# Four gather partitions moved from GpSimd to SyncE and ScalarE in three graph convolutions

## Chip, cores and metric

The program runs on one core of a Trainium2 chip. The metric is the device time of one execution in microseconds. The time before is 11902.84 us, the median of two runs (11900.63 and 11905.05).

## What is computed

The program is a chain of four graph layers on 12,500 nodes with 64 features and 200,000 edges, sorted by destination. The change lies in the last layer, three edge convolutions in a row:

```python
def conv(h, W, b):
    m = jnp.concatenate([h[dst], h[src], edge_attr], axis=1) @ W + b
    return jax.ops.segment_sum(m, dst, num_segments=n_nodes)
h = jax.nn.relu(conv(x, W1, b1))
h = jax.nn.relu(conv(h, W2, b2))
return conv(h, W3, b3)
```

What costs is `h[src]`: for each of the 200,000 edges a row of 64 floats (256 bytes) is read from a table in memory at an index that the data give, and the rows are summed by destination.

## The kernel before

**Tiling.** The edges are laid out as 128 partitions of 1,564 columns each (`P` = 128, `J` = 1564). The columns are worked off in 68 chunks (`NC`) of 23 (`C`). For one column GpSimd issues one indirect DMA: 128 indices, one per partition, are read from `g.src`, and 128 rows of the table `tab3` land in the chunk's buffer `rin`. There are two such buffers, used in turn. In these three convolutions that makes 3 x 1,564 gathers; the same helper `gather_columns` (its issue is L864) also serves the two attention layers ahead of them, from other tables.

**The chunk pipeline of `conv_layer`** (k = 0, 1, 2 is the convolution):

- GpSimd gathers chunk after chunk. Before chunk c it waits until chunk c-2 has been taken out of the buffer (`s_rows` in the helper, `s_in` in `conv_layer`), so it may run a chunk ahead of ScalarE.
- ScalarE's `take(c)` prepares the mask `keeps` (L2098), copies the carry column (L2100), waits for the 23 gathers of the chunk, and copies the rows into `chain` with features outermost (L2106; L2105 copies the edge attributes, in the first convolution alone).
- VectorE runs a scan along the columns (L2244), which sums the rows of one destination.
- ScalarE's `give(c)` waits for the scan and copies the sums out (L2111).
- SyncE waits for that copy (the helper at L90) and stores the chunk (L2068). In the first convolution it also loads edge attributes two chunks ahead (L2049, L2050, L2053).
- In the first 33 chunks ScalarE also does small copies for three node tiles per chunk (L2116 to L2130), between `take` and `give`, for a product on TensorE.

**The order of the work.** Each engine's instructions stand in the order of the code and run in that order; between engines semaphores alone order them. At the start of the program SyncE (L384) and ScalarE (L487) load the weights. Among SyncE's are, for each convolution, parts of 64x64, one of 16x64 and the bias of 1x64, from memory into one partition; among ScalarE's are parts of 16x8x16 and 16x8 (`rel_msg`, `rel_pri`). Up to that point SyncE also stores tables in a loop (L414, L422), where a register operation computes the address ahead of each DMA.

Of the kernel before, what the change touches and what calls it, by code (L numbers as in the profile page):

```python
# [25 lines left out]
U32 = mybir.dt.uint32  # L26

P = 128
# [9 lines left out]
NP = T * P  # L38
# [37 lines left out]
BATCH = 3  # L76
UNIT = 8
ARENA = 25600
SEG = 32
SEGS = -(-J // SEG)  # L80
JP = SEGS * SEG
# [108 lines left out]
def pool_sem(g, name):  # L190


    return g.new_pool_sem(name)
# [660 lines left out]
            v.tensor_copy(g.a2row[:, :], ps_w[:, 260:260 + D])  # L854


def gather_columns(pool, table, idx, rows, s_gath, s_rows):

    for c in range(NC):
        b = c % 2  # L860
        wait(pool, s_rows, c - 1)
        for j in range(C):
            at = c * C + j
            pool.indirect_dma_start(out=rows[b][:, j, :], out_offset=None, in_=table,  # L864
                                    in_offset=bass.IndirectOffsetOnAxis(ap=idx[:, at:at + 1].bitcast(U32), axis=0))\
                .then_inc(s_gath[b], 16)

def store_rows(eng, i, b, rows, width, out, s_rows, s_stored):
# [1104 lines left out]
def conv_layer(nc, ctx, g, a, k, out_rows):  # L1973
# [7 lines left out]
        "rows_turned", "rows_copied", "rows_multiplied", "summed", "relu", "out"))  # L1981
    s_ea = [sem(f"attrs{b}") for b in range(2)]
    s_gath = [pool_sem(g, f"gathered{b}") for b in range(2)]
    s_row = pool_sem(g, "fixed_rows")
    s_blank, s_pair = sem("pair_blank"), sem("pair_in")
    paired = k > 0
# [31 lines left out]
    with ExitStack() as inner:  # L2018
# [4 lines left out]
        ps_o = [bank(f"o{b}") for b in range(ring)]  # L2023
        block = inner.enter_context(nc.Block())

        @block.gpsimd
        def _(pool):
            gather_columns(pool, g.tab3, g.src, rin, s_gath, s_in)

            fix = bass.IndirectOffsetOnAxis(ap=g.fix[:, 0:1].bitcast(U32), axis=0)  # L2030
            pool.wait_ge(s_st, 16 * NC)
            pool.indirect_dma_start(out=row, out_offset=None, in_=table_rows, in_offset=fix).then_inc(s_row, 16)
            pool.wait_ge(s_put, 1)
            pool.indirect_dma_start(out=table_rows, out_offset=fix, in_=row, in_offset=None).then_inc(s_row, 16)
            pool.wait_ge(s_row, 32)
            pool.wait_ge(s_last, 1)

            for n, tiles in enumerate(units):
                for t in tiles:
                    ends = bass.IndirectOffsetOnAxis(ap=g.end_i[:, t:t + 1].bitcast(U32), axis=0)  # L2040
                    pool.indirect_dma_start(out=cat[:, t, 0:width], out_offset=None, in_=table_rows, in_offset=ends)\
                        .then_inc(s_end[n], 16)

        @block.sync
        def _(sp):
            def load_attrs(c):
                b = c % 2
                cols = slice(c * C, c * C + C)
                sp.dma_start(ea[b][0:EVEN, :, :], attrs[0:EVEN, cols, :]).then_inc(s_ea[b], 16)  # L2049
                sp.dma_start(ea[b][EVEN:P - 1, :, :], attrs[EVEN:P - 1, cols, :]).then_inc(s_ea[b], 16)  # L2050
                n = min(LAST - c * C, C)
                if n > 0:
                    sp.dma_start(ea[b][P - 1:P, 0:n, :], last_attrs[:, c * C:c * C + n, :]).then_inc(s_ea[b], 16)  # L2053

            if paired:
                wait(sp, s_blank, 1)
                for half in (slice(0, D), slice(D, P)):
                    sp.dma_start(g.Wkv[half, k - 1, half], a[f"L3_gnn_W{k + 1}"][D:2 * D, :]).then_inc(s_pair, 16)
            wait(sp, s_init, 1)
            if k == 0:  # L2060
                for c in range(2):
                    load_attrs(c)
            for c in range(NC):
                wait(sp, s_in, c + 1)
                if k == 0 and c + 2 < NC:
                    load_attrs(c + 2)
                wait(sp, s_copied, c + 1)
                sp.dma_start(dest[:, c * C:c * C + C, :], rows).then_inc(s_st, 16)  # L2068

            n_out = 0  # L2070
            for n, tiles in enumerate(units):
                t0, t1 = tiles.start, tiles.stop
                done = n + 1
                if k < 2:
                    wait(sp, s_relu, done)
                    sp.dma_start(g.tab3.rearrange("(p t) f -> p t f", t=T)[:, t0:t1, :], g.H[:, t0:t1, :])\
                      .then_inc(s_out, 16)
                    n_out += 1
                else:
                    wait(sp, s_sum, done)  # L2080
                    for p0, p1 in ((0, EVEN), (EVEN, P - 1)):
                        sp.dma_start(out_rows[p0 * T:p1 * T, :].rearrange("(p t) f -> p t f", t=T)[:, t0:t1, :],
                                     g.X[p0:p1, t0:t1, :]).then_inc(s_out, 16)
                        n_out += 1
                    if t0 < REST:
                        whole = min(t1, REST)
                        sp.dma_start(out_rows[(P - 1) * T + t0:(P - 1) * T + whole, :].rearrange("(a t) f -> a t f", a=1),
                                     g.X[P - 1:P, t0:whole, :]).then_inc(s_out, 16)
                        n_out += 1
            wait(sp, s_out, 16 * n_out)  # L2090

        @block.scalar
        def _(act):
            def take(c):
                b, cols = c % 2, slice(c * C, c * C + C)
                act.wait_ge(s_init, 2)
                wait(act, s_rows, c)
                nc.scalar.copy(keeps[:, :, 1:C1], g.keep[:, cols].unsqueeze(1).to_broadcast([P, HF, C])).then_inc(s_flags, 1)  # L2098
                if c:
                    nc.scalar.copy(chain[:, :, 0], chain[:, :, C]).then_inc(s_chained, 1)  # L2100
                    act.wait_ge(s_chained, c)
                act.wait_ge(s_gath[b], (c // 2 + 1) * 16 * C)
                if k == 0:
                    act.wait_ge(s_ea[b], 16 * sum(2 + (LAST > x * C) for x in range(b, c + 1, 2)))
                    nc.scalar.copy(chain[:, D:R3, 1:C1], ea[b].rearrange("p j f -> p f j"))  # L2105
                nc.scalar.copy(chain[:, 0:D, 1:C1], rin[b].rearrange("p j f -> p f j")).then_inc(s_in, 1)  # L2106

            def give(c):
                act.wait_ge(s_rows, c + 1)
                wait(act, s_st, 16 * c)  # L2110
                nc.scalar.copy(rows.rearrange("p j f -> p f j"), chain[:, :, 1:C1]).then_inc(s_copied, 1)  # L2111

            def scale(t):
                b = t % 2
                wait(act, s_tr, t - 1)
                ins = nc.scalar.activation(hd[b][:, 0:D], g.H[:, t, :], ACT.Copy, scale=g.deg[:, t:t + 1])  # L2116
                if k:
                    ins = nc.scalar.copy(hd[b][:, D:K17], g.E17[:, t, :])  # L2118
                ins.then_inc(s_scaled, 1)

            def copy_turned(t):
                b = t % 2
                act.wait_ge(s_tr, t + 1)
                wait(act, s_mm, t - 1)
                nc.scalar.copy(ht[b][0:K_Z, 0:P], ps_t[b][0:K_Z, 0:P]).then_inc(s_ht, 1)  # L2125

            def copy_z(t):
                b = t % 2
                act.wait_ge(s_mm, t + 1)
                nc.scalar.copy(z[:, t, :], ps_o[b][:, 0:D]).then_inc(s_z, 1)  # L2130

            scale(0)
            for c in range(NC):
                take(c)
                for t in range(c * BATCH, min(c * BATCH + BATCH, T)):
                    if t + 1 < T:
                        scale(t + 1)
                    copy_turned(t)
                    if t:
                        copy_z(t - 1)  # L2140
                if c * BATCH < T <= c * BATCH + BATCH:
                    copy_z(T - 1)
                give(c)

            def relu(q):
                tiles = units[q]
                act.wait_ge(s_sum, q + 1)
                h = g.H[:, tiles[0]:tiles[-1] + 1, :].rearrange("p t f -> p (t f)")
                nc.scalar.activation(h, h, ACT.Relu).then_inc(s_relu, 1)

            depth = P if paired else K_T
            for q, tiles in enumerate(units):
                n = len(tiles) * P // (2 if paired else 1)
                act.wait_ge(s_ctr, q + 1)
                wait(act, s_cmm, q - ring + 1)
                nc.scalar.copy(ht[q % ring][0:depth, 0:n], ps_t[q % ring][0:depth, 0:n]).then_inc(s_cht, 1)  # L2156
                if q and k < 2:
                    relu(q - 1)
            if k < 2:
                relu(len(units) - 1)  # L2160
# [161 lines left out]
```

## Time and profile before

| | |
|---|---|
| runs, median | 11902.84 us |
| profiled execution, span | 13242.4 us (the program's rows fill it; no time around it is listed) |
| GpSimd busy | 9106.3 us, 69% |
| VectorE busy | 4015.6 us, 30% |
| ScalarE busy | 3476.7 us, 26% |
| TensorE busy | 1352.0 us, 10% |
| gathers at L864 | 7,820, of which 4,692 in the three convolutions |
| one gather in the convolutions | 0.95 us, and 0.30 us to the next |

The profiled execution is longer than the runs: with the recorder on, the program takes 13242.4 us. Rows are compared with rows, and the sum is carried over to the runs by the ratio of the two. A span's share of busy time is a mean over stages. In the three convolutions, from about 6,100 us to the end, one engine is nearly always issuing and the others wait for it most of the time; the rows further down show it.

### The profile page before, as it was taken

Reading aid. Unit: us, or ns where it says so; the run is one execution under the profiler, and the core shown is the slowest. Engines: PE = TensorE matmul, PEld = TensorE weight load, DVE = VectorE, ACT = ScalarE, POOL = GpSimd, SP = SyncE. Lnnn points to the kernel's source line nnn. Section 1 sums busy time; section 2 is a strip of 40 time slices with the busy share of each in tenths; the row PEclk is TensorE's granted clock in tenths of the full one; section 3 lists DMA queues with packets and bytes.
Section 4 is the critical chain, followed back from the end, with each engine's and each line's share of the span. In section 5 each row is a group of like instructions: output and inputs, shape, how many; then the busy total and the mean of one; then the engine's idle time right before and its main releaser. Section 6 shows DMA issues by size and latency. Waiting matters only on the chain. (4 is left out here: it accounts for less than half of the span.)

```text
span 13242.4 us, 37433 instructions
## 1 busy us (share of the span) xinstructions
PE 1352.0 (10%) x6735; PEld 1005.3 (8%) x6735; DVE 4015.6 (30%) x5472; ACT 3476.7 (26%) x4561; POOL 9106.3 (69%) x8728
## 2 busy tenths in 40 slices
PE   5200000020000000395000000200000000000000
PEld 3100000010000000273000000200000000000000
DVE  2255555544445544695111111011111101111110
ACT  2333223312222222375232222122211212221121
POOL 3677777767777776402777777577777767777776
PEclk7655555555555555697555555555555555555555
DMA  7333333313333333001222222111111111111111
GB/s 277 133 97 97 98 95 95 100 34 90 98 95 94 94 99 81 14 1 32 61 58 61 58 58 60 40 50 46 49 46 46 49 39 50 46 49 46 46 49 42
DMA packets 404823, 919.05 MB, mean 69 GB/s; under 512 B 171046, under 2 KB 195277, under 8 KB 389496
## 3 DMA queue, kind: packets, MB, share of 16 engines
q0 software_dynamic: 278944, 386.91, 13.3%
q1 hardware_dynamic: 121832, 529.42, 10.9%
q14 instruction: 175, 1.43, 0.0%
q10 hardware_dynamic: 3824, 0.50, 0.0%
q8 instruction: 48, 0.79, 0.0%
HBM read 456.45 MB, written 459.77 MB: 69 GB/s over the span
## 5 line engine op out<-in xcount | busy, mean ns | idle before, releaser
L864 POOL DMA_INDIRECT arena<-tab,src x6256 | 6549.8, 1047 | 2894.4 <-issue 2101.0
L2244 DVE TENSOR_TENSOR_SCAN arena<-cv_keep,arena 128x768 f32<-128x768 f32 (+1 forms) x476 | 752.0, 1627 | 5757.2 <-issue 4526.3
L864 POOL DMA_INDIRECT arena<-tab,spread x1564 | 1644.1, 1051 | 518.5 <-issue 518.5
L2106 ACT COPY arena<-arena 128x1472 f32<-128x1472 f32 x204 | 545.3, 2673 | 3003.9 <-DMA arena<-tab,src 3003.9
L2111 ACT COPY arena<-arena 128x1472 f32<-128x1472 f32 (+1 forms) x204 | 588.3, 2884 | 551.8 <-DVE arena L2244 431.2
L1089 PE MATMUL e_t<-ident,arena 128*68 128x128 f32 (+1 forms) x2 | 0.8, 397 | 4433.5 <-PEq L1433 2223.3
L2168 PE MATMUL cv_t<-ident,arena 128*81 128x128 f32 (+1 forms) x294 | 137.9, 469 | 2917.7 <-ACT arena L2118 1528.3
L2105 ACT COPY arena<-arena 128x368 f32<-128x368 f32 x68 | 55.3, 813 | 1353.7 <-issue 1325.1
L2182 PE MATMUL cv_t<-ident,arena 128*64 128x128 f32 (+1 forms) x3 | 1.3, 425 | 3391.1 <-ACT arena L2111 3391.1
L951 ACT ACTIVATE ae_prob<-arena 128x92 f32<-128x92 f32 x68 | 17.1, 251 | 1228.8 <-remote 1152.7
L1089 PEld LDWEIGHTS e_t<-ident,arena 128*68 128x68 f32 (+1 forms) x2 | 0.3, 134 | 4433.9 <-issue 4433.9
L1502 DVE TENSOR_TENSOR arena<-arena,ge_small 128x23 f32<-128x23 f32 x68 | 13.3, 195 | 1064.8 <-DMA arena<-tab,src 1064.8
L1883 DVE TENSOR_SCALAR arena<-arena 128x448 bf16<-128x448 f16 x1252 | 324.8, 330 | 37.4 <-PE po_u L1766 20.4
L1766 PE MATMUL po_u<-arena,Hn 128*128 128x448 bf16 x1564 | 300.6, 354 | 291.4 <-DVE Hn L1873 291.4
L1025 DVE TENSOR_TENSOR arena<-arena,ae_prob 128x1472 f32<-128x1472 f32 x68 | 260.1, 3824 | 220.3 <-issue 217.2
L1465 ACT ACTIVATE ge_decay<-arena 128x768 f32<-128x768 f32 x68 | 56.4, 830 | 1015.4 <-issue 944.1
L992 DVE TENSOR_TENSOR_SCAN ae_work<-ae_keep,arena 128x768 f32<-128x768 f32 x136 | 240.1, 1765 | 224.2 <-remote 146.5
L1766 PE MATMUL po_u<-arena 128*128 128x448 bf16 x1564 | 298.9, 352 | 1.0 <-DVE arena L1883 1.0
L943 ACT ACTIVATE ae_work<-arena 128x768 f32<-128x768 f32 x136 | 208.5, 1533 | 300.7 <-DVE arena L1037 287.5
L2168 PEld LDWEIGHTS cv_t<-ident,arena 128*81 128x81 f32 (+1 forms) x294 | 53.9, 184 | 2953.8 <-ACT arena L2118 1538.3
L1034 DVE TENSOR_TENSOR_SCAN arena<-ae_work,arena 128x768 f32<-128x768 f32 x136 | 238.9, 1757 | 115.3 <-ACT ae_work L943 103.4
L1506 DVE TENSOR_TENSOR arena<-arena,ge_small 128x1472 f32<-128x1472 f32 x68 | 258.7, 3805 | 0.2 <-issue 0.2
(370 smaller groups left out, 6943.0 us busy)
## 6 DMA issues: line engine op xcount, KB each, us to landing
rows<-arena SPq DMA_DIRECT2D x68, 1506.5 KB
arena<-tab,src POOLq DMA_INDIRECT x6256
rows3b<-arena SPq DMA_DIRECT2D x136, 736.0 KB
rows<-arena SPq DMA_DIRECT2D x68, 920.0 KB
rows<-arena SPq DMA_DIRECT2D x68, 828.0 KB
tab<-arena SPq DMA_DIRECT2D x49, 1024.0 KB
q_start<-arena SPq DMA_DIRECT2D x32, 1564.0 KB
arena<-q_start SPq DMA_DIRECT2D x68, 736.0 KB
```

The source lines that it names most:

```text
L864: pool.indirect_dma_start(out=rows[b][:, j, :], out_offset=None, in_=table, in_offset=bass.IndirectOffsetOnAxis(ap=idx[:, at:at + 1].bitca ...
L943: return nc.scalar.activation(works.rearrange("p (h d) j -> p h d j", h=HH), args[:, 0, :, h0:h0 + HH].rearrange("p j h -> p h j").unsquee ...
L992: v.tensor_tensor_scan(out=work[:, :], data0=keep[:, :], data1=qts[:, x * HF * C1:(x + 1) * HF * C1], initial=0.0, op0=ALU.mult, op1=ALU.a ...
L1025: v.tensor_tensor(mix[:, :, 1:C1].rearrange("p (h d) j -> p j h d", h=H), kv[:, :, D:2 * D].rearrange("p j (h d) -> p j h d", h=H), prob.u ...
L1034: ins = v.tensor_tensor_scan(out=part, data0=work[:, :], data1=part, initial=0.0, op0=ALU.mult, op1=ALU.add)
L1506: v.tensor_tensor(peak[:, :, 1:C1].rearrange("p f j -> p j f"), r[:, :, D:2 * D], pre.unsqueeze(2).to_broadcast([P, C, D]), ALU.mult).then ...
L1766: ins = nc.tensor.matmul(ps_u[:, x, 0:half], wide[c % 2][:, x * P:x * P + P, j], ring[:, n % RING, :], start=(n == 0), stop=(n == J - 1))
L1883: v.tensor_scalar(ring[:, n % RING, :], iota_hi, hi[:, n:n + 1], None, ALU.is_equal).then_inc(s_hot, 1)
L2106: nc.scalar.copy(chain[:, 0:D, 1:C1], rin[b].rearrange("p j f -> p f j")).then_inc(s_in, 1)
L2111: nc.scalar.copy(rows.rearrange("p j f -> p f j"), chain[:, :, 1:C1]).then_inc(s_copied, 1)
L2168: nc.tensor.transpose(ps_t[b][0:K_Z, 0:P], hd[b][:, 0:K_Z], g.ident[:, :]).then_inc(s_tr, 1)
L2244: ins = v.tensor_tensor_scan(out=part, data0=keep[:, 0:(f1 - f0) * C1], data1=part, initial=0.0, op0=ALU.mult, op1=ALU.add)
```

## The change

A constant gives the number of partitions that GpSimd gathers in each convolution: 127, 124 and 126. The rest are fetched row by row. SyncE takes the first one or two of them, ScalarE what is left: partition 127 by SyncE in the first convolution; 124 and 125 by SyncE, 126 and 127 by ScalarE in the second; 126 and 127 by SyncE in the third. For each partition and chunk, 23 indices are read from `g.src` into registers of the issuing engine, in two instructions (12 and 11), and for each index a DMA brings one row of 64 floats from `tab3` to its place in `rin`. These DMAs signal four semaphores `s_side` in turn, and `take` waits for them too. Chunks 0 and 1 are fetched ahead of the chunk loop, chunk c+2 at the end of chunk c: on SyncE behind the store, on ScalarE behind `give`, after a wait for its own `take`.

```diff
+GATHERED = (127,124,126)
...
+def fetch_rows(nc, eng, engine, table, idx, c, partitions, dest, signal):
+
+    for p in partitions:
+        for j in range(0, C, 12):
+            n = min(12, C - j)
+            _, values = nc.values_load_multi_w_load_instructions(
+                idx[p:p + 1, c * C + j:c * C + j + n], engines=[engine], min_val=0, max_val=NP - 1,
+                skip_runtime_bounds_check_because="row numbers of the edge list, as the indirect gathers use them")
+            for x, value in enumerate(values):
+                eng.dma_start(dest[p:p + 1, j + x, :], table[bass.ds(value, 1), :]).then_inc(signal, 16)
+
-def gather_columns(pool, table, idx, rows, s_gath, s_rows):
+def gather_columns(pool, table, idx, rows, s_gath, s_rows, n=P):
...
-            pool.indirect_dma_start(out=rows[b][:, j, :], out_offset=None, in_=table,
-                                    in_offset=bass.IndirectOffsetOnAxis(ap=idx[:, at:at + 1].bitcast(U32), axis=0))\
+            pool.indirect_dma_start(out=rows[b][0:n, j, :], out_offset=None, in_=table,
+                                    in_offset=bass.IndirectOffsetOnAxis(ap=idx[0:n, at:at + 1].bitcast(U32), axis=0))\
...
+    n_gathered = GATHERED[k]
+    s_side = [sem(f"side{n}") for n in range(4)]
...
+        of_sp = range(n_gathered, min(n_gathered + 2, P))
+        of_act = range(n_gathered + 2, P)
...
-            gather_columns(pool, g.tab3, g.src, rin, s_gath, s_in)
+            gather_columns(pool, g.tab3, g.src, rin, s_gath, s_in, n_gathered)
...
+            for c in range(2):
+                fetch_rows(nc, sp, mybir.EngineType.SP, g.tab3, g.src, c, of_sp, rin[c % 2], s_side[c % 4])
             for c in range(NC):
                 wait(sp, s_in, c + 1)
                 if k == 0 and c + 2 < NC:
                     load_attrs(c + 2)
                 wait(sp, s_copied, c + 1)
                 sp.dma_start(dest[:, c * C:c * C + C, :], rows).then_inc(s_st, 16)
+                if c + 2 < NC:
+                    fetch_rows(nc, sp, mybir.EngineType.SP, g.tab3, g.src, c + 2, of_sp, rin[c % 2], s_side[(c + 2) % 4])
...
                 act.wait_ge(s_gath[b], (c // 2 + 1) * 16 * C)
+                act.wait_ge(s_side[c % 4], (c // 4 + 1) * 16 * C * (P - n_gathered))
...
             scale(0)
+            for c in range(2):
+                fetch_rows(nc, act, mybir.EngineType.Activation, g.tab3, g.src, c, of_act, rin[c % 2], s_side[c % 4])
             for c in range(NC):
                 take(c)
...
                 give(c)
+                if c + 2 < NC:
+                    act.wait_ge(s_in, c + 1)
+                    fetch_rows(nc, act, mybir.EngineType.Activation, g.tab3, g.src, c + 2, of_act, rin[c % 2],
+                               s_side[(c + 2) % 4])
```

ScalarE's rows in the second convolution, late in the chunk loop, before: `give` of a chunk (L2111), then `take` of the next (L2098, L2100, L2106).

```order
L2106 COPY arena<-arena 128x64x23
L2111 COPY arena<-arena 128x64x23
L2098 COPY cv1_keep<-keep 128x32x23
L2100 COPY arena<-arena 128x64
L2106 COPY arena<-arena 128x64x23
L2111 COPY arena<-arena 128x64x23
```

At the same place in the changed program the lines are numbered 22 higher (L2133 is `give`, L2128 the copy of gathered rows); ISA is a register operation, here the one that turns an index into an address.

```order
L2119 COPY cv1_keep<-keep 128x32x23
L2121 COPY arena<-arena 128x64
L2128 COPY arena<-arena 128x64x23
L2133 COPY arena<-arena 128x64x23
L863 TENSOR_LOAD src
L867 ISA
L867 DMA arena<-tab3 1x64
```

After these come the other 45 pairs of ISA and DMA with three more TENSOR_LOADs among them, 96 instructions in all, and then again L2119, L2121 and L2128: they stand between `give` of one chunk and `take` of the next, where nothing stood before.

SyncE's rows in the second and third convolution before were stores alone (L2068, `rows3b<-arena`, 68 in a row). In the changed program the same 96 instructions stand between two stores; this is the place of one store (now L2087) in the second convolution.

```order
L867 ISA
L867 DMA arena<-tab3 1x64
L2087 DMA rows3b<-arena 128x1472
L863 TENSOR_LOAD src
L867 ISA
L867 DMA arena<-tab3 1x64
```

In the first convolution SyncE has half of that, 48 instructions for one partition. GpSimd's order is unchanged; its gathers read and write fewer partitions. SyncE's program grows from 605 listed rows to 17,058 and ScalarE's from 4,260 to 10,788.

## Rows read from the trace of the kernel before

**Rows 1.** Page: span, then busy us (share) and instructions per engine

```profile
span 13242.4 us, 37433 instructions
PE 1352.0 (10%) x6735; PEld 1005.3 (8%) x6735; DVE 4015.6 (30%) x5472; ACT 3476.7 (26%) x4561; POOL 9106.3 (69%) x8728
```

**Rows 2.** Page, costliest groups: count, busy us, mean ns, idle before, releaser

```profile
L864 POOL DMA_INDIRECT arena<-tab,src x6256 | 6549.8, 1047 | 2894.4 <-issue 2101.0
...
L864 POOL DMA_INDIRECT arena<-tab,spread x1564 | 1644.1, 1051 | 518.5 <-issue 518.5
```

**Rows 3.** Timeline of GpSimd, second convolution: start us, us, [idle before <-releaser]

```profile
8999.32 0.95 POOL L864 DMA_INDIRECT arena<-tab,src  x1 [0.30 <-issue]
9000.58 0.95 POOL L864 DMA_INDIRECT arena<-tab,src  x1 [0.30 <-issue]
9001.83 0.95 POOL L864 DMA_INDIRECT arena<-tab,src  x1 [0.30 <-issue]
```

**Rows 4.** Timeline of ScalarE, second convolution, one late chunk

```profile
9710.17 2.67 ACT L2106 COPY arena<-arena 128x1472 f32<-128x1472 f32 x1 [22.60 <-DMA arena<-tab,src]
9716.38 2.67 ACT L2111 COPY arena<-arena 128x1472 f32<-128x1472 f32 x1 [3.54 <-DVE arena L2244]
9718.86 0.87 ACT L2098 COPY cv_keep<-keep 128x736 f32<-128x736 f32 x1
9719.67 0.35 ACT L2100 COPY arena<-arena 128x64 f32<-128x64 f32 x1
9742.38 2.68 ACT L2106 COPY arena<-arena 128x1472 f32<-128x1472 f32 x1 [22.36 <-DMA arena<-tab,src]
```

**Rows 5.** Groups of ScalarE, second convolution (8500 to 10725 us)

```profile
L2111 ACT COPY arena<-arena 128x1472 f32<-128x1472 f32 x68 | 181.9, 2675 | 168.7 <-DVE arena L2244 129.3 <-issue 39.4
L2106 ACT COPY arena<-arena 128x1472 f32<-128x1472 f32 x68 | 181.9, 2674 | 1502.1 <-DMA arena<-tab,src 1502.1
```

**Rows 6.** Timeline of SyncE's queue, one chunk of the first convolution

```profile
7043.69 0.33 SPq L2049 DMA_DIRECT2D arena<-in_edge_attr_dram  x1
7044.06 0.43 SPq L2050 DMA_DIRECT2D arena<-in_edge_attr_dram  x1
7044.54 0.25 SPq L2053 DMA_DIRECT2D arena<-in_edge_attr_dram  x1
7051.39 0.36 SPq L2068 DMA_DIRECT2D rows<-arena  x1
```

**Rows 7.** Waits of SyncE's queue, second convolution: us in total, times, longest

```profile
SPq L90 <- ACT arena L2111: 1016.0, 32, 38.1
```

**Rows 8.** Groups of GpSimd: scatter of 4-byte rows

```profile
L1638 POOL DMA_INDIRECT s_start<-small,start_i x98 | 101.1, 1032 | 29.9 <-issue 29.9
```

**Rows 9.** Timeline of SyncE's queue: bias of 1x64, then 64x64, 64x64, 16x64

```profile
421.95 0.28 SPq L384 DMA_DIRECT2D Wt<-in_L_gnn_b_dram  x1
422.27 0.47 SPq L384 DMA_DIRECT2D Wz<-in_L_gnn_W_dram  x1
422.78 0.60 SPq L384 DMA_DIRECT2D Wt<-in_L_gnn_W_dram  x1
423.42 0.58 SPq L384 DMA_DIRECT2D Wz<-in_L_gnn_W_dram  x1
```

**Rows 10.** The same, in the loop with register operations between DMAs

```profile
197.34 0.34 SPq L422 DMA_DIRECT2D tab<-arena  x1
197.88 0.39 SPq L414 DMA_DIRECT2D q_start<-arena  x1
202.39 0.35 SPq L422 DMA_DIRECT2D tab<-arena  x1
202.96 1.00 SPq L414 DMA_DIRECT2D q_start<-arena  x1
```

**Rows 11.** Timeline of ScalarE's queue: DMAs of 16 partitions

```profile
9.90 0.45 ACTq L487 DMA_DIRECT2D arena<-in_L_gnn_rel_pri_dram  x1
10.38 0.44 ACTq L487 DMA_DIRECT2D arena<-in_L_gnn_rel_att_dram  x1
```

**Rows 12.** A lone gather, and DMA busy tenths in 40 slices of 8342.4:8345.4

```profile
8342.40 0.95 POOL L2032 DMA_INDIRECT arena<-rows,fix  x1 [16.46 <-DMA rows<-arena]
DMA  0000000000000000000006942300000000000000
```

**Rows 13.** DMA of 9048.2:9049.45, one gather: packets; share of 16 engines

```profile
DMA packets 32, 0.03 MB, mean 26 GB/s; under 512 B 16, under 2 KB 16, under 8 KB 32
q0 software_dynamic: 32, 0.03, 13.9%
```

## Prediction

> **What bounds the kernel now.** I read the page first: GpSimd is busy 69% of the span, no other engine over 30% [rows 1]. A GpSimd row of about 1.05 us stands 7,820 times at L864, one per gathered column, and nothing released most of its idle time but its own issue [rows 2]. So the part to look at is `gather_columns`, and there the three `conv_layer` calls, 1,564 gathers each. The timeline of GpSimd shows the beat: a row of 0.95 us, 0.30 us of issue, 1.25 us from one to the next [rows 3]. A chunk of 23 gathers lasts 32.2 us: in the timeline of ScalarE the copy L2106, which waits for a chunk's rows, starts at 9710.17 and at 9742.38 [rows 4]. Between two such copies ScalarE sits idle: 1502.1 us over the 68 chunks of the second convolution, 22.1 us each, all until the gather's DMA lands [rows 5]. SyncE too has nearly the whole chunk free: one store of 0.36 us, in the first convolution three loads of about 1 us together [rows 6], and waits of 1016.0 us at 32 stops, 31.7 us each [rows 7]. So GpSimd sets the time, ScalarE has 22 us a chunk to give and SyncE 31.
>
> **The change, part by part.** All of this is in the profiled execution's time, 13242.4 us; the runs' median is 11902.84, 0.899 of it, and I carry the sum over by that ratio.
>
> *Fewer partitions per gather.* No row of before gathers other than 128 rows. What rows do show is that bytes don't matter: gathers of 512-byte rows take 1051 ns, scatters of 4-byte rows 1032 ns [rows 2, 8]. So the 0.95 us is either fixed for the instruction (gain 0, and I see no reason for a loss but the one under the rivals), or goes by rows: 0.95/128 = 7.4 ns a row, 11.6 us per row over 1,564 gathers. One, four and two rows are taken off: 81 us at the most. With nothing to tell the two apart I take the middle, 3.7 ns a row: 6 us in the first convolution, 12 us in the third; in the second it shortens a chunk by 4 x 23 x 3.7 ns = 0.3 us.
>
> *What a row costs SyncE or ScalarE.* Each is a register operation (ISA) and a DMA of 1x64. SyncE has issued just such a DMA: 0.28 us, the next one 0.32 us after its start [rows 9]. With a register operation before the next DMA the gap behind a DMA grows from 0.04 to 0.20 us: 0.34 us at 197.34, the next at 197.88 [rows 10]. So 0.28 + 0.20 = 0.48 us. ScalarE's shortest DMAs of before are of 16 partitions, 0.44 to 0.45 us each and 0.48 us apart [rows 11], so its row lies between 0.32 us (SyncE's bare spacing) and 0.48 + 0.16 = 0.64; SyncE took 0.58 us for 16x64 [rows 9], so ScalarE isn't the slower issuer, and I take 0.48 for it too.
>
> *Reading the indices.* Two TENSOR_LOADs per row and chunk (12 and 11 numbers). None stands in before. Bounds: 0.16 us, a register operation's gap, and 1.6 us, what a lone gather needs from its start at 8342.40 to its first packet, in slice 22 of the 40 of 75 ns [rows 12]. I take 0.8. The Trainium skill ("DMA: Bandwidth & Descriptors", Latency and other measured facts) gives a floor of about 600 ns for such a load; by it, an estimate, ScalarE's fetch below would be 24.5 us and the forecast 11,900; no run here shows it yet.
>
> *SyncE.* First convolution: 23 x 0.48 + 2 x 0.8 = 12.6 us a chunk beside 1.4 us of its own: hidden in 31.7. Second and third: 46 x 0.48 + 4 x 0.8 = 25.3 us, hidden too, with 6 us left. Its fetch for chunk c+2 stands behind the store of chunk c, a whole chunk ahead of its use.
>
> *ScalarE, second convolution.* The same 25.3 us now stand between `give(c)` and `take(c+1)`. Ahead of `take` nothing else may run, so the keep copy (0.87 us), the carry copy (0.35), the wait for the gather and L2106 all queue behind the fetch; behind L2106 wait DVE's scans, the store, and GpSimd, which may run one chunk ahead. The fetch can start when the copy L2111 is handed over, not when it ends: L2098 starts at 9718.86, before L2111 ends at 9719.05, so the queue runs ahead of the engine [rows 4]. From 9716.38 to 9742.38 are 26.0 us, less 1.2 for the two copies: a window of 24.8 (the same as 22.1 idle + 2.67), and 24.5 with the shorter gathers. The fetch overruns it by 0.8 us. From then on ScalarE sets the beat: 66 chunks x 0.8 = 53 us. The first two fetches, 50.6 us, run before the first `take`, which before came after 32.2: another 18 us that a bound engine does not make up. In the other convolutions ScalarE only gains a wait on a semaphore long passed.
>
> Sum: 13242.4 - 6 - 12 + 53 + 18 = 13295; times 0.899, **11,950 us**, 0.4% more than now.
>
> **The rivals.**
>
> *All of it is hidden.* If a row on ScalarE costs 0.46 us or less, or a load 0.6, the fetch fits and the gathers' gain is left: 0 to 81 us, so 11,830 to 11,903. For it: SyncE's bare spacing of 0.32 [rows 9]. Against: the margin is under 1 us.
>
> *Issue is dearer, and it gets slower.* At 0.64 us a row and 1.6 us a load the fetch is 35.8 us: ScalarE overruns by 11.3 x 66 = 746 us, its start by 40, and SyncE overruns the third convolution's chunk (36.2 against 32) by 4.2 x 66 = 277: 14,299, or 12,850. It is over 2% (265 us) once the fetch takes 28.4 us, at 0.55 us a row. There is another way past 2%: if the recorder slows GpSimd's rows alone and not ScalarE's, the true chunk is 28.9 us, the window 21.2 and the overrun 4.1 x 66 = 271. For it: SyncE's DMAs behind a large one take 1.00 us where they took 0.39 [rows 10], and the fetches stand behind a 736 KB store.
>
> *The gather itself gets slower.* Now a gather is 16 data packets, 32 with the semaphore writes, and 13.9% of 16 engines over 1.25 us, 2.8 us of one engine's time [rows 13]. If 127 rows, which don't divide, all went to one engine and each gather to the same one, the first convolution's beat would be 2.8 instead of 1.25 us: 1564 x 1.55 = 2,424 us, 14,080 in the runs' time. The Trainium skill (same page, Why a DMA increments its semaphore by 16 and not by 1) says that a DMA takes the largest number of engines up to 16 that divides its slowest dimension, so 1, 4 and 14 here, but moves such DMAs from GpSimd round the engines; by that the engines have room and nothing is lost. The rows of 128 can't show it.
>
> *The gather gets much faster,* if its 0.95 us goes by engines served and 127 rows use one. At the extreme (0.06 us an engine) the first convolution would run at SyncE's 14 us a chunk and save 1,240 us, the third 0.12 x 1564 = 190: 11,883 with the second's loss, or 10,680; at half of it about 11,290. Against: a lone gather's packets start on all engines within five slices of 75 ns [rows 12], so serving sixteen engines is no more than a part of the 0.95.
>
> **How the numbers follow.** Chances: forecast 0.35 (its own range 11,890 to 12,140), all hidden 0.27, issue dearer 0.24, gather slower 0.06, gather much faster 0.08. About 2% is what a measurement of this kernel can tell from no change. Faster by more than that comes from the last case alone: 0.08. Slower comes from the third and fourth: 0.30. The rest, 0.62, is within 2%. The range, 11,800 to 12,650, leaves out the last two cases and the dearest end of the third, 0.18 together.
>
> **What would show it.** Right: GpSimd rows at L876 of 0.92 to 0.95 us in all three convolutions; SyncE's fetched rows 0.48 us apart; in the second convolution a chunk of about 33 us with ScalarE's idle time before the copy of gathered rows near zero and GpSimd waiting; in the others chunks of 32 us. Wrong: a gather row that moves by more than 0.05 us with the partition count (last two rivals); GpSimd without waits in the second convolution (hidden); GpSimd waiting in the third too, or ScalarE's rows over 0.55 us apart (dearer).

## The result, and the profile after

The changed kernel takes 16031.83 us (median of 2 runs, 16024.38 to 16039.27) where the kernel before takes 11902.84: a ratio of 1.347, with a 95% interval of 1.343 to 1.351. It is slower by 35%; the prediction said 11,950, at most 12,650.

The page of the changed kernel: span, busy time of the engines, the two groups of gathers (count | busy us, mean ns | idle before), and the queue that GpSimd's DMAs use (packets, MB, share of 16 engines).

```profile
span 16037.4 us, 71314 instructions
PE 1340.6 (8%) x6735; PEld 1003.2 (6%) x6735; DVE 4011.2 (25%) x5472; ACT 3483.5 (22%) x4561; POOL 11391.9 (71%) x8728
...
L876 POOL DMA_INDIRECT arena<-tab,src x6256 | 8983.2, 1436 | 3601.8 <-issue 3381.7
...
L876 POOL DMA_INDIRECT arena<-tab,spread x1564 | 1476.7, 944 | 476.6 <-issue 476.6
...
q0 software_dynamic: 479136, 398.47, 18.9%
```

Against [rows 1] VectorE, ScalarE and TensorE are as busy as they were; GpSimd works 2,286 us more (3,068 more than in the second profile of the kernel before, below). The lines that answer to [rows 2] say which gathers did it: the 1,564 of an attention layer, still of 128 partitions, take 944 ns, while the group that holds the convolutions' has a mean of 1,436.

GpSimd by stage, from the first to the last gather of each convolution in the changed kernel: window, its length in us, GpSimd's busy us (instructions), granted clock, DMA share, GB/s.

```profile
5579.80:10855.70 5275.90, 3972.80 (x1564) 0.50 0.32 26
11013.90:13585.40 2571.50, 2003.56 (x1564) 0.50 0.18 41
13747.30:15847.00 2099.70, 1529.01 (x1564) 0.50 0.19 48
```

The same view of the kernel before, profiled again in the first experiment:

```profile
5584.30:7538.00 1953.70, 1477.40 (x1564) 0.50 0.23 65
7693.60:9647.40 1953.80, 1477.52 (x1564) 0.50 0.19 52
9799.80:11753.50 1953.70, 1477.48 (x1564) 0.50 0.19 52
```

Busy time over 1,564: a gather takes 0.945 us before, and now 2.540 us with 127 partitions, 1.281 with 124 and 0.978 with 126. The stages grow by 3,322, 618 and 146 us, 4,086 of the 4,126 us between the two spans (another 32 follow the last gather). With the 0.30 us to the next gather, as in [rows 3], the beats are 2.846, 1.586 and 1.287 us instead of 1.250, so longer rows account for 1564 x 1.596 = 2,496, 526 and 58 us. What is left is 826, 92 and 88 us, and it has two causes.

The timeline of GpSimd in the first convolution (start us, us, [idle before <-releaser]) shows the 826:

```profile
6988.21 2.54 POOL L876 DMA_INDIRECT arena<-tab,src  x1 [0.30 <-issue]
6991.05 2.53 POOL L876 DMA_INDIRECT arena<-tab,src  x1 [0.30 <-issue]
6998.32 2.54 POOL L876 DMA_INDIRECT arena<-tab,src  x1 [4.74 <-issue]
7001.17 2.54 POOL L876 DMA_INDIRECT arena<-tab,src  x1 [0.30 <-issue]
```

Before the 8th, 15th and 22nd gather of each chunk GpSimd stands still for 3.5 to 5.3 us, and the profile names nothing that releases it: 68 chunks x 3 x 4.05 us above the usual 0.30 = 826. I call these the idle stretches; what ends them shows in the run with more semaphores.

The 92 us in the second convolution are the predicted wait. ScalarE's timeline there; the ACTq row is the issue of 46 fetched rows:

```profile
11526.45 2.68 ACT L2128 COPY arena<-arena 128x1472 f32<-128x1472 f32 x1
...
11532.67 2.67 ACT L2133 COPY arena<-arena 128x1472 f32<-128x1472 f32 x1 [1.35 <-DVE arena L2272]
11535.76 28.93 ACTq L867 DMA_DIRECT2D arena<-tab  x46
11564.79 0.80 ACT L2119 COPY cv_keep<-keep 128x736 f32<-128x736 f32 x1 [29.45 <-issue]
...
11565.91 2.67 ACT L2128 COPY arena<-arena 128x1472 f32<-128x1472 f32 x1
```

The copy of the gathered rows, which before waited 22 us for its gather [rows 4, 5], now comes 39.5 us after the last one with no wait of its own: the fetch has filled the gap. GpSimd's chunk is 23 x 1.586 = 36.5 us, so GpSimd waits up to 4 us. It doesn't do so in every chunk: each fourth fetch is shorter, the copies are then 33 us apart and ScalarE catches up, so that 29 of the 68 chunks start with a wait of more than 1 us. In the third convolution GpSimd waits for SyncE's rows in the same way. Its waits in both (us in total, times, longest):

```profile
POOL arena L876 <- ACT arena L2128: 208.8, 77, 4.0
```

What a fetched row costs, by line: duration in ns, least/median/longest, of the index loads and of the row DMAs.

```profile
L863 SPq TENSOR_LOAD <-src x680: 1035/2813/8357, 5583.2 to 15872.1; - x170
L863 ACTq TENSOR_LOAD <-src x272: 993/2899/3264, 11013.1 to 13577.4; - x136
L867 SPq DMA_DIRECT2D arena<-tab x7820: 237/241/737, 5585.3 to 15879.1; - x196
L867 ACTq DMA_DIRECT2D arena<-tab x3128: 240/241/1057, 11014.3 to 13584.7; - x196
```

The medians of the loads hide two kinds. The same view of ScalarE's four loads for chunk 16 of the second convolution, then of the four for chunk 17:

```profile
L863 ACTq TENSOR_LOAD <-src x4: 1106/1383/1682, 11611.9 to 11631.6; - x4
L863 ACTq TENSOR_LOAD <-src x4: 2789/2930/3065, 11645.5 to 11670.1; - x4
```

So it is throughout: for chunks 0, 4, 8 and so on, whose first number stands at a multiple of four in its row of indices (23 x 16 = 368), ScalarE's loads took 0.99 to 1.89 us, for the other three 2.77 to 3.26. A whole fetch of 46 rows is 25.6 us in the first case and 32.0 to 32.7 in the others. That the place of the first number makes the difference is read from this pattern; no run moved it.

### The profile page after: what moved, and what is told of

Read it like the earlier page. It is cut to its first block and busy times, and to the rows that moved or that the text cites. A ratio compares the mean times of both kernels' runs of the same rounds, so it can differ in the third digit from the quotient of the medians.

```text
span 16037.4 us, 71314 instructions
## 1 busy us (share of the span) xinstructions
PE 1340.6 (8%) x6735; PEld 1003.2 (6%) x6735; DVE 4011.2 (25%) x5472; ACT 3483.5 (22%) x4561; POOL 11391.9 (71%) x8728
## 5 line engine op out<-in xcount | busy, mean ns | idle before, releaser
L876 POOL DMA_INDIRECT arena<-tab,src x6256 | 8983.2, 1436 | 3601.8 <-issue 3381.7
L876 POOL DMA_INDIRECT arena<-tab,spread x1564 | 1476.7, 944 | 476.6 <-issue 476.6
L2128 ACT COPY arena<-arena 128x1472 f32<-128x1472 f32 x204 | 545.5, 2674 | 1473.9 <-DMA arena<-tab 1421.5
L2133 ACT COPY arena<-arena 128x1472 f32<-128x1472 f32 (+1 forms) x204 | 588.5, 2885 | 551.7 <-DVE arena L2272 551.7
L2119 ACT COPY cv_keep<-keep 128x736 f32<-128x736 f32 x204 | 171.4, 840 | 1913.9 <-issue 1912.2
L1518 DVE TENSOR_TENSOR arena<-arena,ge_small 128x1472 f32<-128x1472 f32 x68 | 258.7, 3805 | 0.2 <-issue 0.2
L1546 DVE TENSOR_TENSOR arena<-arena,ge_small 128x1472 f32<-128x1472 f32 x68 | 257.4, 3786 | 0.0
```

Of the source, the lines that this page charges most:

```text
L876: pool.indirect_dma_start(out=rows[b][0:n, j, :], out_offset=None, in_=table, in_offset=bass.IndirectOffsetOnAxis(ap=idx[0:n, at:at + 1].b ...
L1518: v.tensor_tensor(peak[:, :, 1:C1].rearrange("p f j -> p j f"), r[:, :, D:2 * D], pre.unsqueeze(2).to_broadcast([P, C, D]), ALU.mult).then ...
L1546: v.tensor_tensor(mix[:, :, 1:C1].rearrange("p f j -> p j f"), r[:, :, 0:D], prob.unsqueeze(2).to_broadcast([P, C, D]), ALU.mult).then_inc ...
```

## The experiments

Two theories stood after the result. **S**, splitting: a gather runs on k DMA engines, k the largest divisor of its partition count up to 16, and GpSimd's row pays for what falls on one of them. The expectations below count that in pieces, four to each gathered row where k is below 16. The packets of the changed kernel suggested it. **N**, the rival: any gather of fewer than 128 partitions is dear, whatever it divides by. The queue of GpSimd's DMAs in the first convolution of the changed kernel, and of the kernel before run again:

```profile
q0 software_dynamic: 225071, 62.83, 28.2%
q0 software_dynamic: 50016, 51.32, 12.6%
```

Per gather that is 144 packets instead of 32. By the packets' sizes a gather of 127 partitions puts all its data on one engine, in seven packets of 4,096 bytes and one of 3,840, which are 16 and 15 rows of 256 bytes; for each of the 15 other engines there are seven packets of 64 bytes and one of 60, four bytes for each gathered row. Gathers of 124 use four engines (31 rows each), those of 126 use 14 (9 rows each). This is the rule for k that the prediction took from the Trainium skill ("DMA: Bandwidth & Descriptors", Why a DMA increments its semaphore by 16 and not by 1), and the traces agree with it. The cutting in four is not shown by the sizes: 508 quarter rows with 508 single bytes on each of the other engines, and 127 whole rows with four bytes each, give the same packets.

**The kernel before, again.** No edit.

> The kernel before, unchanged, to get a second profile of it. In the profile that the prediction read, a chunk of 23 gathers lasted 32.2 us and the span was 13242 us against runs of 11903; in the profile of the changed kernel the two attention layers, whose code is the same in both, show a chunk of 28.7 us. Theory A (that first profile was of a slower execution): a chunk of 28.7 us in all five gather stages, gather rows of 0.944 us without the rows of 1.1 to 1.9 us, span within 1% of 11,900. Theory B (this program's gathers are always slowed when profiled): 32.2 us and 13,240 us again.

It took 11913.87 us, its profile spans 11911.6, and in all five gather stages a row is 0.945 or 0.946 us and a chunk 28.74 us. Theory A holds: the chunk of 32.2 us [rows 4] belonged to that one execution, and five stages of 68 chunks, 3.46 us each, are 1,176 of the 1,331 us between the two profiles. So the recorder is not what made 13242.4 us, as the section on the time before has it: with it on, the same kernel spans 11911.6, and the factor 0.899 belonged to one execution.

**The smaller gathers without the fetch.**

```diff
-                fetch_rows(nc, sp, ...)       # all four calls, and ScalarE's wait for s_side
```

> Gathers of 127, 124 and 126 partitions as in the change, but nobody fetches the missing partitions: their rows stay what they were, so part of the sums is left out. Theory S (the shape of the gather is the cost): gather rows of 2.54, 1.28 and 0.98 us as in the changed kernel, idle stretches of 4 to 5 us every seventh gather in the first convolution, and about 11,900 + 1564 x (1.60 + 0.34 + 0.04) + 825 = 15,810 us. Theory F (the row fetches of SyncE and ScalarE get in the way of GpSimd): rows of 0.94 us in all three and about 11,900 us.

15803.56 us; rows of 2.540, 1.282 and 0.977 us; stages of 5261.3, 2480.6 and 2005.1 us, idle stretches before the same gathers as in the changed kernel (812 us). So 3,898 of the 4,129 us between the two kernels come from the gathers alone, and the fetch adds 228 to that.

**The fetch without the smaller gathers.**

```diff
-GATHERED = (127,124,126)
+GATHERED = (128, 124, 126)
-            gather_columns(pool, g.tab3, g.src, rin, s_gath, s_in, n_gathered)
+            gather_columns(pool, g.tab3, g.src, rin, s_gath, s_in)
...
-                fetch_rows(nc, sp, ..., rin[c % 2], ...)     # all four calls
+                fetch_rows(nc, sp, ..., spare[c % 2], ...)
```

> The other half alone: all gathers at 128 partitions as before, and in the second and third convolution SyncE and ScalarE fetch the same rows as in the change, into a spare buffer that nobody reads (ScalarE still waits for them). The first convolution is as before. Theory S: gather rows stay at 0.944 us; in the second convolution ScalarE's fetch (46 rows of 0.40 us and four loads of 2.8 us, 29.6 us) with its own work makes a chunk of about 39.4 us instead of 28.7, 66 x 10.7 = 706 us more, and 30 at the start; in the third SyncE's fetch of about 30 us overruns the chunk of 28.7 by 1 to 2 us, 100 us: about 12,740 us. Theory F: gather rows of 0.98 to 1.28 us here too. Third possibility, all hidden once the gathers are fast: 11,900 us.

12695.77 us, 790 more than before. The three stages (columns as above):

```profile
5588.00:7542.00 1954.00, 1477.34 (x1564) 0.50 0.23 65
7697.00:10237.00 2540.00, 1477.32 (x1564) 0.50 0.15 41
10405.00:12503.00 2098.00, 1477.23 (x1564) 0.50 0.18 49
```

GpSimd's busy time is that of the kernel before; the second stage is 585 us longer, with a median chunk of 39.15 us, the third 143. So the fetch overruns a chunk of 28.74 us by 10.4 us on ScalarE, in the median chunk; each fourth chunk, with the quick loads, takes about 33 us. In the changed kernel the same fetch costs only 228 us, because the slower gathers cover most of it.

**Other partition counts, fetch left out.**

```diff
-GATHERED = (127,124,126)
+GATHERED = (113, 122, 120)     # first kernel
+GATHERED = (112, 64, 31)       # second kernel
```

> No fetch; GpSimd gathers 113, 122 and 120 partitions in the three convolutions, the rest of the rows is left out. Theory S in its form for numbers: a gather runs on the largest number k of engines up to 16 that divides the partitions, each row is then cut in four pieces, and the row takes 0.86 us + 3.3 ns for each piece on one engine. 113 is prime, k = 1, 452 pieces: 2.35 us. 122: k = 2, 244 pieces: 1.66 us. 120: k = 15, 32 pieces: 0.96 us. Time about 11,900 + 1564 x (1.40 + 0.72 + 0.02) = 15,250 us, and up to 700 more for idle stretches. Rival R (the cost goes by the remainder over a multiple of 16, or of 8): 113 has remainder 1 and would be near 1 us, 122 remainder 10, 120 is a multiple of 8 and would cost as 128. Rival N (cost goes by the number of rows): all three under 0.95 us.

> No fetch; GpSimd gathers 112, 64 and 31 partitions in the three convolutions, the other rows are left out. Theory S: 112 and 64 are multiples of 16, run on 16 engines with rows uncut and cost what 128 rows cost, 0.945 us; 31 is prime, one engine, 124 pieces, as many as 124 partitions gave on four engines, so 1.27 us although only a quarter of the rows are moved. Time 11,905 + 1564 x 0.33 = 12,420 us. Rival N (cost per row, as half of my prediction's term assumed): rows of 0.83, 0.47 and 0.23 us and about 9,900 us; at half of that slope 10,900 us.

The first took 16038.34 us, the second 12299.80. Stages of the first, then of the second:

```profile
5584.00:10299.00 4715.00, 3683.01 (x1564) 0.50 0.32 28
10456.00:13721.00 3265.00, 2595.12 (x1564) 0.50 0.26 32
13874.00:15879.00 2005.00, 1527.66 (x1564) 0.50 0.18 49
```

```profile
5579.00:7502.00 1923.00, 1444.98 (x1564) 0.50 0.24 63
7657.00:9541.00 1884.00, 1406.89 (x1564) 0.50 0.15 41
9695.00:12140.00 2445.00, 1967.99 (x1564) 0.50 0.15 27
```

N falls: 112 and 64 partitions are cheaper than 128. The rival R of the first expectation falls too: 113, one more than a multiple of 16, takes 2.355 us and not 1. S holds over all ten counts in this form: 0.86 us and 13.2 ns for each gathered row on one engine (the slope from 126 and 127 partitions, 9 and 127 rows an engine: 1.562 us / 118; a quarter of it, 3.3 ns, is the expectations' price of a piece). The counts that 16 divides lie 0.013 to 0.028 us below that line, and the cutting in four isn't needed for any of the ten.

| partitions | k | rows an engine (partitions / k) | row, us | 0.86 + 0.0132 x rows |
|---|---|---|---|---|
| 64 | 16 | 4 | 0.900 | 0.913 |
| 112 | 16 | 7 | 0.924 | 0.952 |
| 128 | 16 | 8 | 0.945 | 0.966 |
| 120 | 15 | 8 | 0.977 | 0.966 |
| 126 | 14 | 9 | 0.978 | 0.979 |
| 124 | 4 | 31 | 1.281 | 1.269 |
| 31 | 1 | 31 | 1.258 | 1.269 |
| 122 | 2 | 61 | 1.659 | 1.665 |
| 113 | 1 | 113 | 2.355 | 2.352 |
| 127 | 1 | 127 | 2.540 | 2.536 |

31 partitions cost what 124 do and a third more than 128. The idle stretches appeared with 113 (before the 9th and 17th gather, 4 us, and in 60 of the 68 chunks 1.3 us before the 2nd) and with 122 (before the 17th, 3 us), not with 120, 124, 126, 31 or the counts that 16 divides.

**Shorter rows, and two semaphores.** 127 partitions in all three convolutions.

```diff
-            pool.indirect_dma_start(out=rows[b][0:n, j, :], out_offset=None, in_=table,
+            to, of = rows[b][0:n, j, :], table
+            if width:                                    # 16 in the second, 32 in the third convolution
+                to, of = rows[b][0:n, j, 0:width], table.rearrange("n (a f) -> (n a) f", f=width)
+            pool.indirect_dma_start(out=to, out_offset=None, in_=of,
...
-                .then_inc(s_gath[b], 16)
+                .then_inc(other[b] if other and j % 2 else s_gath[b], 16)     # first convolution
```

> No fetch; 127 partitions in all three convolutions, the other rows are left out. First convolution: the gathers of a chunk signal two semaphores in turn instead of one. Second: rows of 16 floats (64 bytes) from the same table seen as shorter rows, third: rows of 32 floats, so part of the data is left out there. On the idle stretches before the 8th, 15th and 22nd gather of a chunk: if they come from counting on one semaphore, they move or go (825 us less); if from the queued pieces alone, they stay where they are. On the pieces: if a row is cut into pieces of 64 bytes, the gather of 16 floats has 127 pieces and takes 1.28 us, that of 32 floats 254 and 1.70 us, about 17,140 us in all (16,300 without the idle stretches); if every row is cut in four whatever its length, 2.54 us in all three and about 21,900 us.

21011.23 us. The three stages:

```profile
5583.00:10335.00 4752.00, 3973.05 (x1564) 0.50 0.36 29
10492.00:15596.00 5104.00, 3970.66 (x1564) 0.50 0.44 15
15749.00:20850.00 5101.00, 3973.07 (x1564) 0.50 0.39 17
```

Rows of a quarter and of half the bytes leave the gather at 2.54 us (3970.66 / 1564). So neither bytes nor a fixed piece of 64 bytes sets the time; the number of rows on the engine does. Whether each is cut in four or not at all this run can't tell, since both give 2.54 us. The packets speak for uncut rows: one of 2,048 bytes takes 147 ns in the mean with 120 partitions, where S as expected cuts it in 32 pieces, and 145 to 148 with 128, where it does not. With two semaphores in turn the stretches came before the 8th, 14th and 20th gather and shrank to 2.6, 1.4 and 1.4 us in the mean: 302 us of them instead of 812.

**More semaphores, and a second wait.** 127 everywhere again.

```diff
-                .then_inc(s_gath[b], 16)
+                .then_inc(more[b][j % len(more[b])] if more else s_gath[b], 16)    # 4, 8, none
+            if j == again:                                # third convolution, j = 4
+                wait(pool, s_rows, c - 1)
```

> No row is fetched (SyncE's and ScalarE's part is left out, so the rows that are not gathered hold nothing of use), and 127 partitions are gathered in all three convolutions. In the first the gathers of a chunk signal four semaphores in turn, in the second eight, in the third one, where GpSimd repeats the wait at the chunk's start, which has long been met, ahead of its fifth gather. Without any stretch a stage would be 1564 x 2.846 = 4,450 us; with one semaphore and one wait it was 5,261, with two semaphores 4,752. If GpSimd waits because too much is outstanding on one semaphore: the idle stretches before the 8th, 15th and 22nd gather shrink below those of two semaphores or go, about 4,500 to 4,650 us with four and 4,450 to 4,500 with eight, and in the third stage nothing changes but the small cost of a wait, 5,260. If GpSimd waits because pieces pile up whatever they signal: all three stages at 5,260. If a wait at the chunk's start sets a count back: in the third stage the stretches come before the 5th plus seven gathers, the 12th and the 19th, two a chunk instead of three, 68 x 4.3 = 290 us less, 4,970. In all: 11,907 - 3 x 1,954 = 6,045 and the sum of the three stages, 20,250 to 21,830.

20216.07 us. The three stages, and the landing time of the first one's gathers (the last number: median us from issue):

```profile
5584.00:10035.00 4451.00, 3973.29 (x1564) 0.50 0.38 31
10192.00:14643.00 4451.00, 3973.45 (x1564) 0.50 0.37 26
14797.00:20054.00 5257.00, 3973.26 (x1564) 0.50 0.31 22
arena<-tab,src POOLq DMA_INDIRECT x1564, 6.2
```

With four semaphores or eight no stretch is left (1564 x 2.846 = 4,451); a second wait changes nothing. The rows on an engine are the same in all three stages, so the stretches hang on how many gathers signal one semaphore, not on rows alone.

What ends a stretch can be read from the packets. In the run without the fetch, GpSimd's timeline, then the DMA busy tenths in 40 slices of 7022.92:7026.92, the stretch itself, and the packets in it:

```profile
7020.19 2.54 POOL L876 DMA_INDIRECT arena<-tab,src  x1 [0.30 <-issue]
7026.92 2.54 POOL L876 DMA_INDIRECT arena<-tab,src  x1 [4.19 <-issue]
...
DMA  0000014495516535492541101010000000000000
...
q0 software_dynamic: 144, 0.04, 23.3%
```

The 144 packets are those of the one gather just before; they end at 7025.74, and 1.18 us later GpSimd goes on. Over all stretches with one semaphore and rows of 256 bytes the time from the end of that gather's last data packet to the next row is 1.18 us in the median with 127 partitions, 1.20 with 113 (9th and 17th gather) and 1.23 with 122. With two semaphores in turn it is 1.16 us from the end of the gather before that one, which signals the same semaphore as the gather that waits. So GpSimd waits there until data has landed. With four in turn the last earlier gather on the same semaphore is four back and has landed by then, which would explain why no stretch is left.

This run also settles whether one DMA engine was the limit: the last data packet comes some 3.1 us after the end of its gather's row in the first thirty gathers of the first stage and in its last thirty. Were the engine slower than the beat, that would grow.

**One index load instead of two.** Fetch to the spare rows, gathers of 128, as above, and:

```diff
-        for j in range(0, C, 12):
-            n = min(12, C - j)
+        for j in range(0, C, C):
+            n = min(C, C - j)
```

> The kernel of fetch only (gathers of 128, the fetched rows go to a spare buffer), with one load of 23 indices per row and chunk instead of two of 12 and 11, so two loads instead of four on each of ScalarE and SyncE. Theory L (a load costs about 2.6 us whatever it brings): the chunk of the second convolution goes from 39.15 to about 34 us, that of the third to GpSimd's 28.7; 12,696 - 66 x 5.1 - 130 = 12,230 us. Rival (a load costs by the number of indices): a load of 5 us and no change, 12,690 us.

12571.73 us, where the fetch with two loads took 12695.77: 124 us or 1% less. Durations as above:

```profile
L863 SPq TENSOR_LOAD <-src x272: 2171/5234/6576, 7691.0 to 12397.1; - x136
L863 ACTq TENSOR_LOAD <-src x136: 2164/5424/6681, 7689.5 to 10154.6; - x136
```

A load of 23 numbers takes about twice as long as one of 12, in each kind of chunk: the price goes by the number, 0.23 us at the median (5.234 / 23) and 0.09 where the load is quick (2.171 / 23), and merging loads saves little. A fetched row follows the one before by 0.40 us (ScalarE) or 0.42 (SyncE) in the median, by 0.44 on average; with its index it costs 0.67 us.

## Why the prediction was wrong

- **The step that failed is "Fewer partitions per gather".** It bounded a gather of fewer rows by 0 and 7.4 ns of gain per row and saw no reason for a loss but a full engine. It drew a line through one point: every gather in the trace had 128 rows. What bytes do was shown rightly [rows 2, 8], and shorter rows confirmed it, but rows on one engine are not bytes. In place of gains of 6 and 12 us in the first and third convolution stood losses of 3,308 and 51 by the smaller gathers alone, and of 527 in the second. The true gain per row, between counts that 16 divides, is 1.3 ns (128 to 112) and 0.5 ns (112 to 64).
- **The rival "the gather itself gets slower" had the sign and, by chance, the beat.** It gave a beat of 2.8 us for the first convolution from one engine's service time [rows 13]; measured 2.846, but as 2.54 us of GpSimd's own row and 0.30 of issue, with the engine keeping up. The time it gave, 14,080, still fell 1,950 us short. Its mechanism therefore had nothing for 124 and 126 partitions, which cost 526 and 58 us in longer rows, nor for the stretches, 826 us. It was given 0.06. The sentence beside it, that by the Trainium skill's rule the engines have room and nothing is lost, was half right: the engines have room, the loss is in GpSimd's row; whether gathers move round the engines no run shows. That the row is GpSimd writing the transfer's descriptors out is argued, not shown; it fits what the Trainium skill says of such rows ("Perfetto Trace Analysis", DMA Instruction — SWDGE (GPSIMD)): they end when the last descriptor is written, not when the data has moved. The trace agrees, with data 3.1 us behind the row's end.
- **Index loads were mis-sized.** Taken at 0.8 us, with bounds of 0.16 and 1.6; measured medians 2.8 and 2.9, and 0.99 to 1.89 for each fourth chunk. Both bounds were from other kinds of operation, and the upper one did not hold. With the quick loads the fetch was 25.6 us, close to the forecast's 25.3; with the others 32. The Trainium skill's floor of about 600 ns ("DMA: Bandwidth & Descriptors", Latency and other measured facts) is a floor indeed, the shortest being 0.99 us, but no price.
- **The row was sized rightly:** 0.48 us taken, 0.44 measured on average; its DMA of 0.241 us is that of [rows 9], 0.28, or less.
- **ScalarE's overrun was the right mechanism at the wrong size.** 0.8 us a chunk was forecast; 10.4 is what a chunk of 28.74 us leaves in the median, and 3 behind the slower gathers, where each fourth chunk makes some of it up. Two terms made it: four loads of 2 us more each, and a chunk read as 32.2 us from the first profile. The prediction had named that second risk and its 28.9 us, and then carried everything over by 0.899 all the same. SyncE, called hidden in the third convolution with 6 us left, overran too: 88 us there, 143 behind gathers of 128. The rival "issue is dearer" was nearer: it put the fetch at 35.8 us and the time at 12,850; the fetch alone measured 12,696, and in the changed kernel its issue runs from the end of one chunk's work to the next copy, 32 us with the first load beside L2133.
- **Of the signs to look for,** the first was decisive: a gather row that moves by more than 0.05 us with the partition count. It moved by 1.6.

## What to carry to other kernels

Keep the partition count of a GpSimd gather at a multiple of 16: 112 or 64 of 128 save next to nothing, while 127 nearly triple the row and 31 cost more than 128. What counts is the rows left to one engine: 120 or 126 partitions, on 15 and 14 engines, cost only 0.03 us more than 128. A bound on an operation that the trace holds in one size only must be open upwards. Rows taken off a gather can't pay for themselves here: 16 of 128 save 0.021 us per gather, and fetching one of them by itself costs 0.67 us. If the place of the first number is what makes index loads quick, a chunk of 24 columns instead of 23 would make all of them so; no run tried it.

## What the runs showed of the hardware

- A gather of n partitions puts its data on k engines, k the largest divisor of n up to 16, and GpSimd's row is 0.86 us and 13.2 ns for each gathered row on one of them, within 0.03 us for the ten counts from 31 to 128, and for rows of 64, 128 and 256 bytes alike (2.54 us with 127). Whether rows are cut into pieces on the way is not shown.
- The idle stretches: 3 x 4.05 us a chunk with 23 gathers of 127 partitions on one semaphore, 302 us a stage with two, none with four. GpSimd goes on about 1.2 us after an earlier gather's data has landed. They begin after 7 x 127 = 889, 8 x 113 = 904 and 16 x 61 = 976 rows an engine; one gather more would make 1,016, 1,017 and 1,037. Room for between 976 and 1,016 outstanding rows an engine would fit these three. With 113 partitions the 2nd gather of a chunk, the ninth after the last stop, waited until 1.18 us after the last gather of the chunk before, which signals another semaphore, had landed. What the room is, and why 127 partitions seem to count from the start of the chunk, stays open.
- Reading row numbers into registers costs 0.23 us each in three chunks of four, in loads of 12, 11 and of 23, and 0.08 to 0.17 in the fourth, whose first number stands at a multiple of four. In the first convolution, beside the gathers of 127 partitions, SyncE's loads are longer, 4.19 us in the median:

```profile
L863 SPq TENSOR_LOAD <-src x136: 1467/4190/8357, 5583.2 to 10728.6; - x136
```
